# Clustered attention and the small MLP: one joined program, and an opening in a new order

## The chip, the cores and the metric

The kernel runs on one core of one Trainium2 chip. The metric is the time of the device in microseconds (us). Before the change it is 1465.72 us, the median of three runs (1465.66 to 1467.35).

The five engines of the core work side by side, each through its own list of instructions in order: TensorE (PE), VectorE (DVE), ScalarE (ACT), GpSimd (POOL) and SyncE (SP), which only issues DMAs here. They wait for each other by semaphores.

## The reference

The input is 8 batches of 512 tokens with 128 features. Two blocks follow each other.

```python
x = x + attn_block(layernorm(x))           # block 1, on the normalised input n
# inside: n1 = layernorm(n, ln1); q, k, v = n1 @ Wq, Wk, Wv   (16 heads of 8)
#   qb, kb = softmax(q @ Whq), softmax(k @ Whk)               (32 clusters)
#   a = softmax(q k^T / sqrt(8) + 0.1 * qb kb^T) v @ Wo + n
#   a + relu(layernorm(a, ln2) @ W1 + b1) @ W2 + b2           (the small MLP, 512 wide)
x = x + local_ffn(layernorm(x))            # block 2, two layers of windowed
#   attention (8 heads of 64, window 64, rotary) and a gated MLP
```

## The kernel before, in words

`build` calls three stages: `clustered_attention`, `mlp_and_turn` and `local_layers`. Each is a block of its own: every engine has to end its list of one block before any of them begins the next.

**Clustered attention.** A tile is 128 tokens of all features, a batch is 4 tiles. All engines walk the same slots, from -59 to 265 (`over_slots`). A batch has 32 slots of attention; in slot n ScalarE takes one exponential of 128x1024 scores (L670, unit n of 256), TensorE makes the scores of unit n+1 (L410) and the preliminary scores of unit n+12 (L430), of which VectorE takes row maxima (L618), and every second slot TensorE weights the values (L444). The scores have one pair of PSUM banks, so exponential n and scores n+1 take turns. Beside it each tile is prepared in 8 slots: normalise (`scale_input`, GpSimd L751), transpose, project q, k, v (L462) and the two products with the cluster weights (L467), softmax over the clusters, and a split of each number into a leading and a remaining half-precision part, written to `stack_tok` (L782 to L791 on GpSimd; for the queries of the first four tiles `whole_query_chain` on VectorE, L571 to L591). Four transposing DMAs per tile (L827) bring `stack_tok` to `stack`, in the order of `STACK_PARTS`: first half of the heads of the keys, of the queries, then the second halves. `stack_tok` is a single buffer: the next tile's split waits for these DMAs. The first preliminary scores wait for the keys' first half of four tiles and the queries' of three. Small products share three PSUM banks, the bench, in the order of `BENCH_ORDER`.

**The opening.** SP loads the 8 batches of X and then 19 weights, and TensorE waits for all of them before it folds the hash weights into `w_cl` (L378). VectorE takes the statistics of all 32 tiles first (L514, L517). `standardise` (ACT, L658) writes the normalised Z of tiles 4 to 31 in the slots -55 to -28.

**The small MLP.** `mlp_and_turn` works by whole batches: centre (ACT L980), transpose (PE L1049), first product (L1057), ReLU (ACT L995), second product (L1066), addition and statistics (DVE L931 to L946), square root (ACT L1002), normalise (ACT L1010), transpose back (PE L1076) and copy to XT (ACT L1016). Its SP list loads the tables and the first layer's weights of the local stage. The hidden values have four PSUM banks, the outputs two.

## Time and profile before

| what | before |
|---|---|
| median of three runs | 1465.72 us |
| time of the profiled execution | 1465.65 us |
| its span, first to last instruction | 1463.8 us |
| TensorE busy | 1268.3 us, 87% |
| VectorE busy | 1090.7 us, 75% |
| ScalarE busy | 998.3 us, 68% |
| GpSimd busy | 822.2 us, 56% |
| first preliminary scores of a batch | at 70.80 us |
| block of the small MLP begins and ends | 621.77 and 702.2 us |

Busy time is the sum of an engine's instructions, and its share is taken over the whole span; a stage in which the engines wait for each other shows only in a view cut by time. The 1.85 us between the profiled execution's time and its span lie before the first and after the last instruction.

### The profile page before, as it was taken

How to read it: one execution, taken by the hardware profiler on the slowest of the kernel's cores; microseconds unless marked ns; L12 is line 12 of the kernel's file. 1: busy time of each engine (PE TensorE's matmuls, PEld its weight loads, DVE VectorE, ACT ScalarE, POOL GpSimd, SP SyncE). 2: the span in 40 equal slices, each digit the busy share in tenths (PEclk: the TensorE clock that was granted, in tenths of full speed). 3: DMA queues.
4: the chain of work that ended last, by engine and by line, in shares of the span. 5: the costliest groups of instructions: out<-in, count | busy, mean ns of one | idle time of the engine just before them, and what ended most of it. 6: DMA issues, size and time to landing. Idle time of an engine off the chain costs nothing.

```text
span 1463.8 us, 27861 instructions
## 1 busy us (share of the span) xinstructions
PE 1268.3 (87%) x9636; PEld 643.2 (44%) x9636; DVE 1090.7 (75%) x1943; ACT 998.3 (68%) x2313; POOL 822.2 (56%) x1005
## 2 busy tenths in 40 slices
PE   3378989998998988679589999998988999999898
PEld 1112222222222322157256666665534666666554
DVE  4778888888888877223489999995447999999644
ACT  4236766676666666577488999985337999999632
POOL 3666666667766640022577888870028888877200
PEclk9659999999999999989799999999999999999999
DMA  3523333343334330010111111110101111111001
GB/s 103 110 42 65 73 59 65 60 79 58 66 58 73 65 59 1 1 57 1 37 26 27 27 30 27 28 27 2 47 15 42 31 30 27 27 27 31 1 17 41
DMA packets 161120, 60.87 MB, mean 42 GB/s; under 512 B 139691, under 2 KB 152789, under 8 KB 160981
## 3 DMA queue, kind: packets, MB, share of 16 engines
q1 hardware_dynamic: 160980, 59.09, 19.1%
q8 instruction: 78, 1.28, 0.4%
q14 instruction: 62, 0.50, 0.1%
HBM read 8.60 MB, written 2.10 MB: 7 GB/s over the span
## 4 chain that ended last, share of the span: by engine, by line
PE 29%; ACT 11%; DVE 7%; issue 4%; POOL 2%; ACTq 0%; DVEq 0%; POOLq 0%
ACT la_s L1735 8%; PE la_ring L1360 6%; PE la_ring L1372 3%; PE la_s L1393 3%; PE la_pT L1467 3%; DVE la_prob L1624 2%; PE la_pT L1406 2%; PE la_m L1539 2%; PE la_ring L1455 1%; PE la_pT L1457 1%; PE la_s L1455 1%; PE la_s L1457 1%; ACT la_v_own L1777 1%; PE la_s L1385 1%; PE la_o L1422 1%
## 5 line engine op out<-in xcount | busy, mean ns | idle before, releaser
L618 DVE TENSOR_REDUCE row_max<-max_ps 128x2 f32<-128x1024 f32 x256 | 312.9, 1222 | 70.6 <-PE max_ps L430 69.2
L670 ACT ACTIVATE prob<-scores_ps 128x1024 f32<-128x1024 f32 x256 | 262.2, 1024 | 147.8 <-PE scores_ps L410 144.3
L1735 ACT ACTIVATE la_s<-la_s,la_bias,la_inv 128x128 f32<-128x128 f32 x512 | 223.4, 442 | 7.0 <-DVE la_bias L1612 7.0
L1886 POOL TENSOR_TENSOR la_turned<-la_raw,lw_rot 128x1024 f32<-128x1024 f32 x64 | 150.9, 2358 | 115.6 <-PE la_ring L1372 70.1
L1360 PE MATMUL la_ring<-lw_wqkv,la_hT 128*128 128x512 f32 x384 | 202.4, 638 | 15.3 <-DVE la_swapped L1587 6.7
L410 PE MATMUL scores_ps<-stack 128*128 128x512 f16 x512 | 155.7, 386 | 42.0 <-ACT prob L670 41.1
L1892 POOL TENSOR_TENSOR la_turned<-la_turned,la_swapped 128x1024 f32<-128x1024 f32 x64 | 150.7, 2355 | 5.0
L444 PE MATMUL heads_ps<-prob,v_pad 128*32 128x512 f32 x1024 | 137.2, 608 | 1.1 <-ACT prob L670 1.1
L430 PE MATMUL max_ps<-stack 24*128 24x512 f16 x512 | 102.5, 397 | 31.2 <-DVE row_max L618 18.5
L410 PEld LDWEIGHTS scores_ps<-stack 128*128 128x128 f16 x512 | 34.2, 97 | 208.7 <-ACT prob L670 161.3
L1587 DVE TENSOR_TENSOR la_swapped<-la_ring,lw_rot 128x256 f32<-128x256 f32 x256 | 90.8, 415 | 33.3 <-ACT la_raw L1746 23.8
L1735 ACT ACTIVATION_READ_ACCUMULATOR la_s<-la_s,la_bias,la_inv 128x1 f32 x512 | 110.9, 217 | 0.0
L776 POOL TENSOR_TENSOR cl<-cl,cl_inv 128x512 f32<-128x512 f32 x60 | 63.0, 1050 | 85.1 <-DVE cl_inv L559 85.1
L1372 PE MATMUL la_ring<-mlp_ident,la_turned 128*128 128x128 f32 x512 | 82.5, 285 | 12.9 <-DVE la_swapped L1587 11.9
L1360 PEld LDWEIGHTS la_ring<-lw_wqkv,la_hT 128*128 128x128 f32 x384 | 65.4, 197 | 63.8 <-issue 40.0
L1624 DVE TENSOR_TENSOR la_prob<-la_s,la_inv_sum 128x512 f32<-128x512 f32 x128 | 88.5, 691 | 4.8 <-DVE la_inv_sum L1620 0.5
L1406 PE MATMUL la_pT<-mlp_ident,la_prob 128*128 128x128 f32 x512 | 78.6, 276 | 10.5 <-DVE la_prob L1624 8.4
L1372 PEld LDWEIGHTS la_ring<-mlp_ident,la_turned 128*128 128x128 f32 x512 | 58.6, 143 | 61.6 <-ACT la_qT L1759 23.8
L960 POOL TENSOR_TENSOR mlp_base<-X,Z 128x512 f32<-128x512 f32 x8 | 10.2, 1270 | 132.6 <-POOLq L257 87.9
L1746 ACT ACTIVATE la_raw<-la_ring 128x512 f32<-128x512 f32 x128 | 70.6, 589 | 19.0 <-PE la_ring L1360 17.4
L767 POOL TENSOR_TENSOR cl_half<-cl 128x256 f32<-128x256 f32 x60 | 44.0, 733 | 69.4 <-ACT cl L703 69.4
L467 PE MATMUL bench<-w_cl,xnT 128*128 128x512 f32 x128 | 77.7, 694 | 4.6 <-ACT xnT L675 4.1
(177 smaller groups left out, 2765.7 us busy)
## 6 DMA issues: line engine op xcount, KB each, us to landing
la_v_back<-la_v_own SPq DMA_DIRECT2D x112, 128.0 KB, 2.3
X<-in_x SPq DMA_DIRECT2D x8, 256.0 KB, 5.4
stack<-stack_tok SPq DMA_TRANSPOSE x128, 3.2
out<-X SPq DMA_DIRECT2D x8, 256.0 KB, 2.3
lw_wqkv<-in_wqkv SPq DMA_DIRECT2D x2, 768.0 KB, 4.8
stack<-shift_row SPq DMA_DIRECT2D x64, 2.0 KB
lw_rot<-in_rot SPq DMA_DIRECT2D x2, 512.0 KB, 6.5
lw_w<-in_fw SPq DMA_DIRECT2D x2, 341.0 KB
```

The costliest lines, as they stand in the source:

```text
L410: mm = nc.tensor.matmul(scores_ps[:, i, :], stack[:, par, 1, h, kt * P:(kt + 1) * P], stack[:, par, 0, h, :], start=True, stop=True)
L430: mm = nc.tensor.matmul(max_ps[:, e, :], stack[rows, b % 2, 0, 2 * pair + e, qt * P:(qt + 1) * P], stack[rows, b % 2, 1, 2 * pair + e, :], ...
L444: mm = nc.tensor.matmul(heads_ps[32 * j:32 * j + 32, :], v_pad[:, par, kt, 4 * g + j, :], prob[:, c % 4, j, :], start=(kt == 0), stop=(kt ...
L618: nc.vector.tensor_reduce(row_max[:, grp % 2, w // 2, :, w % 2], max_ps[:], AX.X, ALU.max).then_inc(max_made, 1)
L670: nc.scalar.activation(prob[:, c % 4, 2 * pr:2 * pr + 2, :], scores_ps[:], ACT.Exp, scale=1.0 / LOGIT_SCALE).then_inc(exp_made, 1)
L1360: mm = nc.tensor.matmul(ring_ps[:, r % 2, :], hT[:, b % 2, t * P:(t + 1) * P], wqkv[:, at:at + INNER], start=True, stop=True)
L1372: mm = nc.tensor.transpose(ring_ps[:, r % 2, c * P:(c + 1) * P], turned[:, T % 2, SIDE[use], c * P:(c + 1) * P], ident[:])
L1406: mm = nc.tensor.transpose(pT_ps[:, j, :], prob[:, T % 2, j, :], ident[:])
L1624: nc.vector.tensor_tensor(prob[:, T % 2, heads], s_ps[:, heads], inv_sum[:, heads].unsqueeze(2).to_broadcast([P, 4, KEYS]), ALU.mult).then ...
L1735: ins = nc.scalar.activation(s_ps[:, place(h), :], s_ps[:, place(h), :], ACT.Exp, bias=bias[:, T % 2, h:h + 1], scale=inv[:, T % 4, h:h + ...
L1886: nc.gpsimd.tensor_tensor(spun, raw[:, T % 2].rearrange("p s (h f) -> p s h f", f=LD), rot[:, T % TPB, :, 0, :].unsqueeze(2).to_broadcast( ...
L1892: nc.gpsimd.tensor_tensor(turned[:, T % 2], turned[:, T % 2], swapped[:], ALU.add).then_inc(added_rot, 1)
```

## The change

The small MLP is no longer a block. Its pieces run in the list of clustered attention: one batch per 7 slots, from slot 226 on (`mlp_at`), past the last slot of attention to slot 309. Its buffers lie in the half of `stack` that batch 6 has left, its PSUM banks are those that attention leaves: bench banks 1 and 2 (from slot 223 the bench's own uses keep to bank 0), then those of the row maxima, the scores and the heads. The square root of the two inner normalisations becomes a power of -0.5 on GpSimd. The two tables and the q, k, v weights of the first local layer are loaded in the opening.

In the opening the first batch goes ahead: SP loads batch 0, the four weights of the fold, six weights, and only then the other batches and the rest. VectorE takes the statistics of batch 0, then of batches 1 to 3, and of 4 to 7 after the first tile's cluster scores; `standardise` moves to slots -31 to -4. For the first four tiles ScalarE scales the input and writes the leading parts of keys and queries, VectorE and GpSimd write the rests, the queries' half a tile period later than the keys', and the four DMAs go keys, keys, queries, queries.

```diff
 FIRST_STEP, LAST_STEP = -10, 18
 FIRST_SLOT = FIRST_STEP - LEAD_PREP
-LAST_SLOT = B * SLOTS + 10
+LAST_SLOT = B * SLOTS + 16
+MLP_SLOT = B * SLOTS - 30
+MLP_STEPS = 7
+ONE_BANK = MLP_SLOT - 3
+MC = MLP // P
...
 STACK_PARTS = ((1, 0), (0, 0), (1, 1), (0, 1))
-BENCH_ORDER = {}
+FIRST_PARTS = ((1, 0), (1, 1), (0, 0), (0, 1))
+BENCH_BANKS = 3
+BENCH_ORDER, BENCH_BANK, BENCH_BEFORE, BENCH_LAST = {}, {}, {}, {}
 for _n in range(FIRST_SLOT, LAST_SLOT):
     for _u in (*bench_uses(_n)[0], *bench_uses(_n)[1]):
         BENCH_ORDER[_u] = len(BENCH_ORDER)
-BENCH_LIST = list(BENCH_ORDER)
-BENCH_BANKS = 3
+        _banks = BENCH_BANKS if _n < ONE_BANK else 1
+        BENCH_BANK[_u] = BENCH_ORDER[_u] % _banks
+        BENCH_BEFORE[_u] = BENCH_LAST.get(BENCH_BANK[_u])
+        BENCH_LAST[BENCH_BANK[_u]] = _u
...
-                 (w_qT[:, 0, :], a["wqT"]), (w_qT[:, 1, :], a["wkT"]),
-                 (w_hash[:, 0, :], a["whq"]), (w_hash[:, 1, :], a["whk"]),
-                 (w_o[:], a["wo"]), (ln1[:, 0:1], a["ln1_g"]), (ln1[:, 1:2], a["ln1_b"])] + mlp_loads
+        fold_loads = [(w_qT[:, 0, :], a["wqT"]), (w_qT[:, 1, :], a["wkT"]),
+                      (w_hash[:, 0, :], a["whq"]), (w_hash[:, 1, :], a["whk"])]
+        loads = [(ident[:], a["ident"]), (ln1[:, 0:1], a["ln1_g"]), (ln1[:, 1:2], a["ln1_b"]),
+                 (w_qkv[:, 0, :], a["wq"]), (w_qkv[:, 1, :], a["wk"]), (w_qkv[:, 2, :], a["wv"])]
+        late_loads = [(ident16[:], a["ident16"]), (w_o[:], a["wo"])] + mlp_loads
...
         shift_made = sem("shift_made")
         shift_row_made = sem("shift_row_made")
         shift_placed = sem("shift_placed")
+        mlp_ident, w1, w2, b1, ln2, b2_rows = (weights[x] for x in ("ident", "w1", "w2", "b1", "ln2", "b2_rows"))
...
+        def mlp_at(n):
+
...
+        def h_bank(b, c):
+            if b < 2:
+                return bench_ps[:, 1, :]
+            return max_ps[:, c % 2, :] if b == 2 or c < 2 else scores_ps[:, c % 2, :]
+
+        def o_bank(b):
+            return bench_ps[:, 2, :] if b < 4 else heads_ps[:] if b % 2 == 0 else bench_ps[:, 0, :]
...
         @block.tensor
         def _(pe):
-            pe.wait_ge(w_loaded, 16 * len(loads))
+            pe.wait_ge(fold_loaded, 16 * len(fold_loads))
             for i in range(2):
                 nc.tensor.matmul(max_ps[:, i, :], w_qT[:, i, :], w_hash[:, i, :],
                                  start=True, stop=True).then_inc(folded, 1)
+            pe.wait_ge(w_loaded, 16 * len(loads))
...
+            def first_product(b, c):
+                pe.wait_ge(yT_made, b + 1)
+                if b == 0 and c == 0:
+                    bench_is_read(BENCH_LAST[1])
+                elif b < 2:
+                    pe.wait_ge(h_made, MC * b + c)
+                elif b == 2 and c < 2:
+                    pe.wait_ge(max_made, B * SLOTS)
+                elif b == 3 and c >= 2:
+                    pe.wait_ge(exp_made, B * SLOTS)
+                elif b < 4:
+                    pe.wait_ge(h_made, MC * b + c - 1)
+                else:
+                    pe.wait_ge(h_made, MC * (b - 1) + c + 1)
+                nc.tensor.matmul(h_bank(b, c), w1[:, c * P:(c + 1) * P], yT[:, b % 2, :],
+                                 start=True, stop=True).then_inc(h_filled, 1)
...
+            def second_product(b, half):
+                pe.wait_ge(h_made, MC * (b + 1))
+                if b < 4:
...
+                elif b == 4:
+                    pe.wait_ge(heads_moved, B * 4)
+                elif b == 5:
+                    bench_is_read(BENCH_LAST[0])
+                else:
...
+            def mlp_slot(n):
+                m, k = mlp_at(n)
+                if k == 0 and batch_or_none(m + 1) is not None:
+                    turn_input(m + 1)
+                if k == 0 and batch_or_none(m - 3) is not None:
+                    turn_output(m - 3)
+                if 1 <= k <= MC and batch_or_none(m) is not None:
+                    first_product(m, k - 1)
+                if k > MC and batch_or_none(m - 1) is not None:
+                    second_product(m - 1, k - MC - 1)
...
         @block.vector
...
+
+            def input_stats(b):
...
+                for T in range(b * TPB, (b + 1) * TPB):
+                    nc.vector.bn_stats(in_stats[:, T, :], X[:, T, :]).then_inc(stats_done, 1)
+                for T in range(b * TPB, (b + 1) * TPB):
+                    dve.wait_ge(stats_done, T + 1)
+                    ins = nc.vector.bn_aggr(moments[:, T, :], in_stats[:, T, :])
+                ins.then_inc(moments_done, 1)
+
...
+            input_variance(0, FIRST)
...
-            dve.wait_ge(dev1_done, 1)
-            nc.vector.reciprocal(R1[:], dev1[:]).then_inc(r1_done, 1)
+            input_scale(0, FIRST)
+            for b in range(1, 4):
+                input_stats(b)
...
+            def query_share(x):
+
+                cluster_sum(x, 0)
                 share = share_of(x, 0)
-                dve.wait_ge(cl_exp_made[0], x + 1)
-                nc.vector.tensor_reduce(cl_sum[:, 0, :], cl[:, x % 2, 0].rearrange("p (h n) -> p h n", n=NB), AX.X,
-                                        ALU.add).then_inc(cl_sum_made[0], 1)
-                invert_sum(x, 0)
                 dve.wait_ge(cl_inv_made[0], x + 1)
                 nc.vector.tensor_tensor(share, share, inverse_of(0), ALU.mult).then_inc(cl_share_made[0], 1)
...
+            def query_rest(x):
                 dve.wait_ge(hi_made[0], x + 1)
-                nc.vector.tensor_tensor(in_stack(0, 1, 2 * DH, DH, 1), feat, in_stack(0, 1, DH, DH, 1), ALU.subtract)
-                nc.vector.tensor_tensor(in_stack(0, 0, 2 * NB, NB, 1), pairs(share), in_stack(0, 0, NB, NB, 1),
-                                        ALU.subtract).then_inc(lo_made[0], 1)
+                nc.vector.tensor_tensor(in_stack(0, 1, 2 * DH, DH, 1), features_of(x, 0), in_stack(0, 1, DH, DH, 1),
+                                        ALU.subtract)
+                nc.vector.tensor_tensor(in_stack(0, 0, 2 * NB, NB, 1), pairs(share_of(x, 0)),
+                                        in_stack(0, 0, NB, NB, 1), ALU.subtract).then_inc(lo_made[0], 1)
...
-                    nc.vector.bn_stats(stats[:, t, :], Z[:, t, :])
+                    nc.vector.bn_stats(stats[:, t, :], Z[:, t, :]).then_inc(tok_stats_done, 1)
+                dve.wait_ge(tok_stats_done, (x + 1) * TPB)
+                for t in range(x * TPB, (x + 1) * TPB):
+                    nc.vector.bn_aggr(in_moments[:, t, :], stats[:, t, :]).then_inc(in_moments_done, 1)
...
+            def mlp_slot(n):
+                m, k = mlp_at(n)
+                if k == 1 and batch_or_none(m + 2) is not None:
+                    input_shift(m + 2)
+                if k == 1 and batch_or_none(m - 2) is not None:
+                    output_shift(m - 2)
+                if k == MLP_STEPS - 1 and batch_or_none(m - 1) is not None:
+                    add_second(m - 1)
...
-                        whole_query_chain(x)
-                    elif x is not None:
+                    if x is not None and (task != cluster_sum or side == 1 or x >= TPB):
                         task(x, side)
+                    if task == cluster_subtract and side == 0 and x == 0:
+                        for b in range(4, B):
+                            input_stats(b)
+                for x in range(TPB):
+                    if x == tile_at_step(n, 11 if x == TPB - 1 else 16):
+                        query_share(x)
+                    if x == tile_at_step(n, 12 if x == TPB - 1 else 18):
+                        query_rest(x)
...
+                    input_variance(1, REST)
+                    nc.vector.scalar_tensor_tensor(out=minus_mean[:, REST], in0=moments[:, REST, 0], scalar=-1.0,
+                                                   in1=r0[:, REST], op0=ALU.mult, op1=ALU.mult
...
         @block.scalar
...
+            def input_dev(part, tiles):
+                act.wait_ge(moments_done, (1, B)[part])
+                nc.scalar.activation(dev[:, tiles], moments[:, tiles, 1], ACT.Sqrt, bias=eps[:, 0:1]
+                                     ).then_inc(dev_done, 1)
...
+            def leading_part(x, side):
+
+                act.wait_ge(cl_share_made[side], x + 1)
+                act.wait_ge(qkv_made, x + 1)
+                if x >= 1:
+                    act.wait_ge(stack_made[side, 0], 16 * x)
+                    act.wait_ge(stack_made[side, 1], 16 * x)
+                else:
+                    act.wait_ge(constants_set, 1)
+                share, feat = pairs(share_of(x, side)), features_of(x, side)
+                nc.scalar.activation(in_stack(side, 0, (0, NB)[side], NB, 2),
+                                     share.unsqueeze(3).to_broadcast([P, H // 2, 2, 2, NB]), ACT.Copy)
+                nc.scalar.activation(in_stack(side, 1, (0, DH)[side], DH, 2),
+                                     feat.unsqueeze(3).to_broadcast([P, H // 2, 2, 2, DH]), ACT.Copy
+                                     ).then_inc(hi_made[side], 1)
...
+                if tile_at_step(n, -10) is not None and tile_at_step(n, -10) < TPB:
+                    scale_input(tile_at_step(n, -10))
+                if 0 <= n - FIRST_SLOT - 28 < NT - TPB:
+                    standardise(n - FIRST_SLOT - 28 + TPB)
                 if s["exp"] is not None:
                     exponentiate(s["exp"])
...
+                if tile_at_step(n, 9) == 1:
+                    input_dev(1, REST)
                 if s["out"] is not None:
                     g = s["out"]
...
+                for x in range(TPB):
+                    if x == tile_at_step(n, 11):
+                        leading_part(x, 1)
+                    if x == tile_at_step(n, 12 if x == TPB - 1 else 17):
+                        leading_part(x, 0)
+                if tile_at_step(n, 9) == 1:
+                    input_dev1(1, REST)
                 if s["att_t"] is not None:
                     nc.scalar.activation(att_T[:], filled("att_t", s["att_t"]), ACT.Copy).then_inc(att_T_made, 1)
                 if s["max"] is not None and s["max"] % UNITS == UNITS - 1:
...
+            def centre(b):
+                act.wait_ge(in_shift_done, b + 1)
+                if b == 0:
+                    act.wait_ge(scored, (B - 1) * SLOTS)
+                elif b - 1 > 0:
+                    act.wait_ge(turned, b - 1)
+                for i in range(TPB):
+                    T = b * TPB + i
+                    ins = nc.scalar.activation(y[:, b % 2, i, :], Z[:, T, :], ACT.Identity,
+                                               bias=in_shift[:, T:T + 1], scale=in_inv[:, T:T + 1])
...
+            def hidden(b, c):
+                act.wait_ge(h_filled, MC * b + c + 1)
+                if b - 1 > 0:
+                    act.wait_ge(o_filled, 2 * (b - 1))
+                nc.scalar.activation(hid[:, b % 2, c, :], h_bank(b, c), ACT.Relu,
+                                     bias=b1[:, c:c + 1]).then_inc(h_made, 1)
...
+            def normalise(b):
...
+            def take_turned(b):
+                act.wait_ge(out_turned, b + 1)
+                if b == 0:
+                    act.wait_ge(pv_made, B * 16)
+                nc.scalar.activation(XT[:, b, :], bench_ps[:, 1, :], ACT.Copy).then_inc(XT_made, 1)
...
+            def mlp_slot(n):
+                m, k = mlp_at(n)
+                if k == 1 and batch_or_none(m + 1) is not None:
+                    take_yT(m + 1)
+                if 2 <= k < 2 + MC and batch_or_none(m) is not None:
+                    hidden(m, k - 2)
+                if k == MC and batch_or_none(m - 3) is not None:
+                    take_turned(m - 3)
+                if k == MLP_STEPS - 1 and batch_or_none(m + 2) is not None:
+                    centre(m + 2)
+                if k == MLP_STEPS - 1 and batch_or_none(m - 2) is not None:
+                    normalise(m - 2)
...
         @block.gpsimd
...
+            def invert_input(b):
+                at = slice(b * TPB, (b + 1) * TPB)
+                pool.wait_ge(in_moments_done, (b + 1) * TPB)
+                nc.gpsimd.tensor_tensor(in_var[:, at], in_moments[:, at, 1], mlp_eps[:, 0], ALU.add
+                                        ).then_inc(in_var_done, 1)
+                pool.wait_ge(in_var_done, b + 1)
+                nc.gpsimd.tensor_tensor(in_inv[:, at], in_var[:, at], power[:], ALU.pow).then_inc(in_inv_done, 1)
...
+            def invert_output(b):
...
         @block.sync
...
+            def load_input(b):
                 sp.dma_start(X[:, b * TPB:(b + 1) * TPB, :], x_tiles[:, b]).then_inc(loaded[b], 16)
+
...
+            load_input(0)
+            for dst, src in fold_loads:
+                sp.dma_start(dst, src).then_inc(fold_loaded, 16)
             for dst, src in loads:
                 sp.dma_start(dst, src).then_inc(w_loaded, 16)
+            for b in range(1, B):
+                load_input(b)
+            for dst, src in late_loads:
+                sp.dma_start(dst, src).then_inc(late_loaded, 16)
+            for dst, src in early_loads:
+                sp.dma_start(dst, src).then_inc(early_loaded, 16)
...
+                for i, step in enumerate((12, 14, 16, 18)):
+                    x = tile_at_step(n, step)
+                    if x is not None:
+                        turn_stack(x, *(FIRST_PARTS if x < TPB else STACK_PARTS)[i])
 
```

## Rows read from the trace of the kernel before

**Rows 1.** The page's slices: granted TensorE clock, in tenths of full speed.

```profile
PEclk9659999999999999989799999999999999999999
```

**Rows 2.** Busy time by stretch: length, each engine's busy time (instructions), clock, DMA share, GB/s.

```profile
60.00:80.00 20.00, 8.51 (x17) 1.87 (x16) 14.39 (x24) 3.26 (x7) 8.33 (x12) 0.59 0.50 93
...
559.00:594.00 35.00, 28.97 (x181) 8.57 (x183) 24.70 (x30) 21.50 (x27) 0.00 (x0) 1.00 0.00 1
594.00:614.00 20.00, 12.99 (x78) 2.75 (x70) 0.55 (x2) 13.07 (x14) 0.00 (x0) 1.00 0.00 1
614.06:621.77 7.71, 3.45 (x24) 1.96 (x24) 2.11 (x7) 1.19 (x2) 0.00 (x0) 1.00 0.00 0
621.77:637.80 16.03, 8.00 (x16) 3.90 (x17) 3.40 (x36) 9.34 (x19) 5.01 (x4) 0.57 0.40 129
637.80:695.40 57.60, 57.60 (x359) 44.21 (x359) 19.16 (x77) 45.70 (x96) 15.25 (x12) 1.00 0.00 1
695.40:702.50 7.10, 2.16 (x13) 1.34 (x10) 2.29 (x11) 4.09 (x11) 0.00 (x0) 0.71 0.00 1
```

**Rows 3.** Timeline of the opening: start, length, instruction, [idle before <- what ended it].

```profile
15.72 0.43 SPq L813 DMA_DIRECT2D mlp_b_rows<-in_mlp_b_rows  x1
17.94 3.78 PE L378 MATMUL max_ps<-w_hash,w_qT 128*128 128x512 f32 x4 [17.94 <-DMA mlp_b_rows<-in_mlp_b_rows]
21.75 1.08 ACT L652 ACTIVATE w_cl<-max_ps 128x512 f32<-128x512 f32 x2 [3.31 <-PE max_ps L378]
25.05 0.69 DVE L542 TENSOR_REDUCE cl_max<-bench 128x16 f32<-128x512 f32 x1 [6.23 <-PE bench L467]
```

**Rows 4.** Timeline of the third tile's preparation, to the fourth's first instruction.

```profile
48.41 0.68 DVE L542 TENSOR_REDUCE cl_max<-bench 128x16 f32<-128x512 f32 x1
...
52.42 0.63 DVE L571 TENSOR_REDUCE cl_sum<-cl 128x16 f32<-128x512 f32 x1
...
53.69 1.38 POOL L782 CAST stack_tok<-cl 128x1024 f16<-128x1024 f32 x1
...
55.50 1.34 POOL L789 TENSOR_TENSOR stack_tok<-cl,stack_tok 128x512 f16<-128x512 f32 x1
...
58.17 0.68 DVE L542 TENSOR_REDUCE cl_max<-bench 128x16 f32<-128x512 f32 x1
```

**Rows 5.** Timeline: the first preliminary scores.

```profile
70.80 0.61 PE L430 MATMUL max_ps<-stack 24*128 24x512 f16 x2 [7.66 <-DMA stack<-stack_tok]
```

**Rows 6.** The transposing DMAs of 30 to 100 us, by their line.

```profile
L827 SPq DMA_TRANSPOSE stack<-stack_tok x20: 1232/1328/1362, 37.7 to 93.7; - x20
...
DMA to landing us min/median/max: 3.0/3.3/3.9
```

**Rows 7.** Groups to 702 us: instructions, count, busy, mean ns.

```profile
L514 DVE BATCH_NORM_STATS2 in_stats<-X 128x6 f32<-128x128 f32 x32 | 8.3, 265 | 3.3 <-DMA X<-in_x 3.2
```

**Rows 8.** Timeline: nine exponentials in a row late in attention, first and last.

```profile
576.87 1.02 ACT L670 ACTIVATE prob<-scores_ps 128x1024 f32<-128x1024 f32 x1 [1.27 <-PE scores_ps L410]
...
592.00 1.02 ACT L670 ACTIVATE prob<-scores_ps 128x1024 f32<-128x1024 f32 x1 [1.26 <-PE scores_ps L410]
```

**Rows 9.** Timeline: one batch of the small MLP, and one normalisation on ScalarE.

```profile
658.40 1.64 ACT L1010 ACTIVATE mlp_w<-X,mlp_out_shift,mlp_out_inv 128x128 f32<-128x128 f32 x4
...
660.15 0.60 PE L1076 MATMUL mlp_turn_ps<-mlp_ident,mlp_w 128*128 128x128 f32 x4
...
661.02 3.60 PE L1057 MATMUL mlp_h_ps<-mlp_yT,mlp_w 128*128 128x512 f32 x8
...
664.46 3.73 PE L1066 MATMUL mlp_o_ps<-mlp_w,mlp_hid 128*128 128x128 f32 x32
...
668.03 0.60 PE L1076 MATMUL mlp_turn_ps<-mlp_ident,mlp_w 128*128 128x128 f32 x4
```

**Rows 10.** ScalarE's groups, whole span: one of six table loads.

```profile
L703 ACT ACT_TABLE_LOAD x1 | 1.3, 1283 | 0.0
```

**Rows 11.** Timeline: a small GpSimd instruction.

```profile
723.75 0.21 POOL L1871 TENSOR_TENSOR la_newton<-la_inv 128x16 f32<-128x16 f32 x1
```

585 lines of the change are left out of this document (263 added, 322 removed).

## The prediction

> **What bounds the kernel now.** I read the page's slices first, because the shares over the whole span hide stages. TensorE's granted clock is low in three places: the opening, between the stages in the middle, and shortly after [rows 1]. The change touches the first two, so I cut the span by stages [rows 2] and read the timeline in both. The local stage, from 702.5 us on, is over half of the span; of it the change moves only some loads.
>
> The opening is a chain through all engines. TensorE does nothing until the last of 27 loads, issued at 15.72, has landed at 17.94; the cluster weights are ready at 22.83, and VectorE takes the first tile's first maximum at 25.05 [rows 3]. Then one tile follows the other every 9.76 us [rows 4], although no engine is full: at 60 to 80 us TensorE is busy for 8.51 of 20 us, at 0.59 of its clock [rows 2]. The first preliminary scores come at 70.80 and waited for a transposing DMA [rows 5]. Everything of clustered attention hangs on that moment.
>
> In late attention a slot takes 1.89 us (eight slots from 576.87 to 592.00) [rows 8]; it is bound by the turns of ScalarE and TensorE over one pair of score banks, with TensorE idle for 6.0 of 35 us and then for 7.0 of 20 us [rows 2]. At 614.06 the last slot's products begin; until 621.77 there is only the tail of batch 7, TensorE busy for 3.45 us. From 621.77 to 637.80 the MLP starts up at a clock of 0.57, and from 637.80 to 695.40 TensorE is busy all the time at full clock: the stage's body is bound by it [rows 2]. A batch takes 668.03 - 660.15 = 7.88 us: first product 3.44, second 3.57, the two transposes 0.87 together [rows 9]. Last comes a ramp-out of 7.1 us at 0.71 [rows 2].
>
> **The opening, part by part.** Fold and first weights are now DMAs 2 to 11. 15.72 us over 26 issues is 0.60 each, and the last one landed 2.2 us after its issue [rows 3]; so the fifth DMA, which the fold waits for, lands at 5.3 by issue alone, and I take 6.4, since five large transfers share the engines. That is 11.5 us earlier. Three small ScalarE instructions and a transpose now stand between the cluster weights and the first maximum, where they were done in the shade of the DMAs. Each costs between 0.21 [rows 11] and 0.69 [rows 4], 0.8 to 2.8 together; I take 1.3. The first maximum comes at 25.05 - 11.5 + 1.3 = 14.8, a gain of 10.2.
>
> VectorE keeps the statistics of batches 4 to 7 in its list, but now behind the first tile's subtraction: 16 x 0.265 = 4.2 us [rows 7] on the path, as the first tile's sum is queued behind it.
>
> For the tiles after it the old loop is in VectorE's list: from the whole sum at 52.42 to the next tile's maximum at 58.17, 5.75 us of query chain with its waits [rows 4]. It goes to ScalarE (leading parts) and to a later slot. What is late next is the single `stack_tok`: keys' leading part on ScalarE (I take GpSimd's 1.38 for the same elements [rows 4]), rest on GpSimd (1.34 [rows 4] and about 0.6 for its small twin), two DMAs, the second issued 1.33 after the first and landed 3.3 later [rows 6], together 4.6, and 0.3 of handing over: 8.2 us. Below it would be VectorE's own 6.5 or so, above it the old 9.76. ScalarE also carries the 28 `standardise` now beside these tiles, and in tile 1 the square roots of the other 28 tiles: two more table loads of 1.28 each [rows 10], as the exponentials go on before and behind. I take 8.8 for a plain tile, 9.6 for the one with the table loads, and 9.1 for the first (4.9 before its neighbour may start, and 4.2 of statistics): 27.5, against 58.17 - 25.05 = 33.1 before. From the fourth tile's first maximum to the first preliminary scores it was 12.6 (70.80 - 58.17); the keys now pass a longer way (subtraction, VectorE's share of the tile before, GpSimd, ScalarE, GpSimd, DMA), which I sum to 16.1, 3.5 more. Opening: 10.2 + 5.6 - 3.5 = 12.3, taken as 12; first preliminary scores at 58.8. The ends: 16, if a tile takes the 8.2 of the buffer loop and the last way 14; 6, if periods stay at 9.76.
>
> The Trainium skill (ScalarE: Activation LUTs, section on table sets) speaks against this part: exponential and square root are in different sets and should be batched. It gives some 2.7 us per load; the row shows 1.28, and the row decides. By the page's figure the two loads cost 5.3 instead of 2.6, and the opening's gain would be near 10.
>
> **The MLP, part by part.** Its TensorE work to the end of the last second product is 8 x (3.44 + 3.57) + 14 transposes of 0.435 = 62.2 us [rows 9] (the last two transposes back lie in the ramp-out). By slot 256 the new list has done five transposes in, one back, 3.5 first products and two second ones: 2.6 + 12.0 + 7.1 = 21.8.
>
> How much longer do slots 225 to 256 get? TensorE's idle time from 559 to 614 is 13.0 us [rows 2]. If all of it is filled, the stretch grows by 21.8 - 13.0 = 8.8: the floor. Products of 0.86 (a quarter of 3.44) or half second products of 1.79 fit well, as they run while ScalarE takes the exponential of 1.02 [rows 8]. ScalarE's blocks don't: five centrings and one normalisation of 1.64 each [rows 9] stand between two exponentials, where the turn leaves it 1.89 - 1.02 = 0.87 [rows 8], some of that used for shifts and heads. Each adds 0.8 to 1.1, I take 1.0, together 6.0. ReLUs of 0.69 fit in the turn. So 14.8. The upper end is that nothing overlaps: 21.8 + 6.0, near 28.
>
> Behind slot 256 there remain 40.4 us of MLP and 3.45 of attention's tail [rows 2] on TensorE. The tail's waits are now filled, and the transpose in of batches 3 to 6 uses the bank of the outputs until VectorE has added them: 0.9 each (0.69, the size of [rows 4]'s maximum, and a handing over), three of them, 2.7, and 1.5 for waits of the tail in TensorE's list: 4.2. Together 14.8 + 40.4 + 3.45 + 4.2 = 62.9 us from old 614.06 to the end of the last second product, against 695.4 - 614.06 = 81.3: a gain of 18.4. It is the start-up at half clock [rows 2] that goes: TensorE has no gap in front of the MLP, so its clock should stay at 2.4 GHz. The ramp-out stays at 7.1, with a power and an addition on GpSimd in the place of ScalarE's root and VectorE's reciprocal. No row has a power; 0.21 for a small GpSimd instruction [rows 11] and 1.38 for a large one [rows 4] bound it, and I take 0.3 more per pass, counted once: 18.1.
>
> Elsewhere: four aggregations on VectorE and two small GpSimd instructions per batch of attention, in seven batches, next to 1.9 us slots; 0 to 3 us, I take 1.0. The weights loaded early cost nothing, SP and the DMA engines being free there; the tables loaded at the start of the local stage are wanted some 25 us later.
>
> **Sum.** 1465.65 - 12 - 18.1 + 1.0 = **1436.6 us**. The profiled execution is 0.07 below the median and 1.85 over its span; both are kept.
>
> **Rivals.**
> *The opening is bound by ScalarE.* Its list now holds scaling, exponentials, both leading parts, `standardise` and tables, in order; each wait for a DMA holds the next tile's exponential. For it: `stack_tok`'s DMAs land 3.3 us after issue [rows 6]. Against: ScalarE is busy for 3.26 of 20 us there [rows 2]. Periods stay near 10, the gain of the opening falls to 5: 1443.6.
> *The joined slots pack badly.* TensorE's list is in order, so a product that waits for a ReLU holds the scores. Growth of 28: 1449.8. Against: batches 0 and 1 share one hidden bank, but a ReLU ends as the next exponential may begin.
> *They pack well*, growth near the floor of 8.8 and DMAs that land early: 1428.
> *The other side: table loads between exponential and ReLU.* Each of the 13 ReLUs of slots 235 to 256 stands between exponentials. If they need different tables, each costs two loads, 2.57 [rows 10], 33 us in all, and 1470 comes out, slower. It decides from 23 loads on. For it: in the trace no ReLU runs under the exponential's table. Against: in 702 us there are only loads for square root and exponential, though copies and scalings run under both.
> The Trainium skill (ScalarE: Activation LUTs, section on table sets) says that cheap functions such as relu and copy are filler in every set. By that rule this rival falls; the rows agree for the copies and cannot show it for ReLU.
> *It doesn't overlap at all*, because an engine's order holds the MLP behind slot 256: then only the opening's gain and the half-clock start-up remain, 1447; no order in the lists speaks for it.
>
> **Chances.** Forecast with its surroundings (1430 to 1443) 0.58; opening bound by ScalarE 0.15; bad packing or none 0.12; good packing 0.08; table loads 0.04; rest 0.03. About 0.2%, 3 us, is what can be told from no change. Faster 0.92, within 0.2% 0.03, slower 0.05. Range: from the floor of the packing with the best opening, 1425, to bad packing with the forecast's opening, 1451.
>
> **What the new profile would show.** The fold begins at 6 to 7 us; first maximum near 15; first preliminary scores near 59; tiles 8 to 9 us apart. Two more table loads for roots in the opening, none in the joined slots. From slot 225 to 256 some 15 us longer than before; no half clock there; steps of 7.9 to 8.8 us behind it; the local stage begins some 30 us earlier than 702.5 and then runs the same 761 us. It is wrong if the joined slots show a ScalarE that switches tables, a tile period near 10, or a local stage that is longer.

## The result, and the profile after

| | before | changed |
|---|---|---|
| median, 4 runs each | 1466.28 us | 1441.97 us (1439.89 to 1443.88) |
| profiled execution, its span | 1465.65, 1463.83 us | 1443.05, 1441.26 us |

The ratio is 0.9833, 95% interval 0.9816 to 0.9850: 24 us faster, 5.4 above the forecast of 1436.6 and inside its range. A second measurement of the same kernel, in another group of runs, gave 0.9825 (0.9808 to 0.9842). All times compared here are of undisturbed executions; the single other one, 2099.94 us at a mean granted clock of 0.552 (of the version without the power), is left out.

I cut both traces at the same events, each stretch from the start of one instruction to the start of the next one named. Lengths in us; the last two columns belong to the experiments below.

| stretch | before | changed | forecast of the change | measured | three edits |
|---|---|---|---|---|---|
| start to first row maximum | 71.44 | 58.80 | -12 | -12.6 | 58.51 |
| to the first exponential | 24.48 | 24.47 | 0 | 0 | 24.47 |
| exponential 0 to 224 | 459.69 | 461.46 | +1.0 | +1.8 | 461.10 |
| 224 to 255 (joined slots) | 57.38 | 75.85 | +14.8 | +18.5 | 71.42 |
| 255 to the end of the MLP | 89.24 | 57.02 | -32.9 | -32.2 | 54.69 |
| local stage | 761.61 | 763.66 | 0 | +2.0 | 761.10 |

The granted clock of the changed kernel, by slices, against [rows 1]: the half-clock stretch between the stages is shorter, and it is still there.

```profile
PEclk9579999999999999998799999999999999999999
```

Busy time by stretch, as in [rows 2] (length, then the engines' busy times, clock, DMA share, GB/s): tile preparation; joined slots; behind them to the last second product; ramp-out; start of the local stage.

```profile
30.00:50.00 20.00, 9.04 (x15) 3.90 (x14) 14.42 (x29) 18.24 (x38) 8.78 (x11) 0.67 0.68 125
544.73:620.58 75.85, 64.24 (x376) 25.85 (x375) 33.28 (x57) 54.73 (x83) 7.45 (x8) 1.00 0.00 1
620.58:668.40 47.82, 46.47 (x296) 34.94 (x294) 19.22 (x69) 33.49 (x65) 21.62 (x25) 1.00 0.00 1
668.40:677.90 9.50, 2.26 (x9) 1.43 (x8) 2.81 (x11) 4.52 (x11) 3.17 (x4) 0.62 0.00 1
677.90:700.40 22.50, 14.16 (x15) 4.52 (x16) 8.69 (x25) 6.56 (x11) 11.95 (x11) 0.50 0.29 75
```

The MLP's start-up at clock 0.57 [rows 2] is gone: in this trace the clock is 1.00 from the joined slots to the last second product, and TensorE is busy for 46.47 of the last 47.82 us. The opening, in the timeline of the changed kernel, against [rows 3] and [rows 5]:

```profile
6.36 3.78 PE L425 MATMUL max_ps<-w_hash,w_qT 128*128 128x512 f32 x4 [6.36 <-DMA w_hash<-in_whk]
...
13.24 1.49 PE L513 MATMUL bench<-w_qkv,xnT 128*128 128x384 f32 x2
...
16.48 0.69 DVE L674 TENSOR_REDUCE cl_max<-bench 128x16 f32<-128x512 f32 x1 [3.44 <-PE bench L518]
...
24.60 0.63 DVE L674 TENSOR_REDUCE cl_max<-bench 128x16 f32<-128x512 f32 x1
...
33.85 0.68 DVE L674 TENSOR_REDUCE cl_max<-bench 128x16 f32<-128x512 f32 x1
...
43.04 0.68 DVE L674 TENSOR_REDUCE cl_max<-bench 128x16 f32<-128x512 f32 x1
...
58.15 0.61 PE L481 MATMUL max_ps<-stack 24*128 24x512 f16 x2 [6.54 <-DMA stack<-stack_tok]
```

The fold starts as forecast. The steps from tile to tile are 8.1, 9.25 and 9.2 us, 26.6 against a forecast of 27.5 and 33.1 before [rows 3, 4]. The last way, from 43.04 to 58.15, is 15.1 instead of 16.1. The steps of the small MLP behind the joined slots, from the end of one batch's second product to the next, are 11.2, 9.8, 9.0, 8.1 and 7.4 us, where I had written 7.9 to 8.8.

### The profile page after: what moved, and what is told of

Same layout as the page of the kernel before. It is cut to its first block, busy times and chain, and to the rows that moved or that the text cites. A ratio compares the mean times of both kernels' runs of the same rounds, so it can differ in the third digit from the quotient of the medians.

```text
span 1441.3 us, 27920 instructions
## 1 busy us (share of the span) xinstructions
PE 1268.8 (88%) x9636; PEld 643.8 (45%) x9636; DVE 1084.5 (75%) x1927; ACT 1007.7 (70%) x2327; POOL 824.9 (57%) x1020
## 3 DMA queue, kind: packets, MB, share of 16 engines
q8 instruction: 78, 1.28, 0.4%
## 4 chain that ended last, share of the span: by engine, by line
PE 29%; ACT 11%; DVE 8%; issue 4%; POOL 2%; ACTq 0%; DVEq 0%; POOLq 0%
ACT la_s L1859 8%; PE la_ring L1480 6%; PE la_ring L1492 3%; PE la_s L1515 3%; PE la_pT L1589 3%; DVE la_prob L1748 2%; PE la_pT L1528 2%; PE la_m L1663 2%; PE la_ring L1577 2%; PE la_s L1579 1%; PE la_pT L1579 1%; PE la_s L1577 1%; ACT la_v_own L1901 1%; PE la_s L1507 1%; PE la_o L1544 1%
## 5 line engine op out<-in xcount | busy, mean ns | idle before, releaser
L495 PE MATMUL heads_ps<-prob,XT 128*32 128x512 f32 x1024 | 137.9, 611 | 0.0
L1492 PE MATMUL la_ring<-mlp_ident,la_turned 128*128 128x128 f32 x512 | 81.9, 283 | 12.6 <-DVE la_swapped L1711 11.6
L1528 PE MATMUL la_pT<-mlp_ident,la_prob 128*128 128x128 f32 x512 | 78.7, 276 | 11.8 <-DVE la_prob L1748 10.3
L1730 DVE TENSOR_REDUCE la_neg_max<-la_s 128x8 f32<-128x1024 f32 x64 | 77.8, 1216 | 5.4 <-PE la_s L1515 5.4
L481 PEld LDWEIGHTS max_ps<-stack 24*128 24x128 f16 x512 | 24.4, 91 | 128.4 <-DVE row_max L785 85.3
L1528 PEld LDWEIGHTS la_pT<-mlp_ident,la_prob 128*128 128x128 f32 x512 | 59.5, 141 | 49.4 <-DVE la_prob L1748 38.6
```

Source lines behind the costliest of these rows:

```text
L481: mm = nc.tensor.matmul(max_ps[:, e, :], stack[rows, b % 2, 0, 2 * pair + e, qt * P:(qt + 1) * P], stack[rows, b % 2, 1, 2 * pair + e, :], ...
L495: mm = nc.tensor.matmul(heads_ps[32 * j:32 * j + 32, :], v_pad[:, par, kt, 4 * g + j, :], prob[:, c % 4, j, :], start=(kt == 0), stop=(kt ...
L1492: mm = nc.tensor.transpose(ring_ps[:, r % 2, c * P:(c + 1) * P], turned[:, T % 2, SIDE[use], c * P:(c + 1) * P], ident[:])
L1528: mm = nc.tensor.transpose(pT_ps[:, j, :], prob[:, T % 2, j, :], ident[:])
```

## The joined slots, read

TensorE's groups between exponentials 224 and 255, before (555.61 to 612.98 us) and changed (544.73 to 620.58): count, busy, mean ns, idle time before them and what ended it.

```profile
L410 PE MATMUL scores_ps<-stack 128*128 128x512 f16 x62 | 18.7, 384 | 12.5 <-ACT prob L670 11.9
L444 PE MATMUL heads_ps<-prob,v_pad 128*32 128x512 f32 x128 | 17.0, 604 | 0.0
```

```profile
L459 PE MATMUL scores_ps<-stack 128*128 128x512 f16 x62 | 18.7, 383 | 7.3 <-ACT prob L890 7.1
L495 PE MATMUL heads_ps<-prob,XT 128*32 128x512 f32 x128 | 17.0, 605 | 0.0
L582 PE MATMUL bench<-stack,mlp_w 128*128 128x512 f32 x16 | 8.6, 619 | 3.4 <-ACT stack L985 3.4
L597 PE MATMUL bench<-mlp_w,stack 128*128 128x128 f32 x64 | 7.8, 275 | 0.0
L481 PE MATMUL max_ps<-stack 24*128 24x512 f16 x40 | 7.8, 384 | 0.5 <-DVE row_max L785 0.5
```

Before, TensorE was busy for 44.55 us and idled 12.8, nearly all of it in front of the scores. Now it idles 75.85 - 64.24 = 11.6: only 5.2 us of the wait for the exponential are filled, and 3.4 of a new wait stand beside it. That is a first product waiting for the ReLU that empties the one hidden bank of batches 0 and 1. A centring is seen from both sides at 563 us:

```profile
562.40 0.60 PE L459 MATMUL scores_ps<-stack 128*128 128x512 f16 x2
...
563.02 1.63 ACT L970 ACTIVATE stack<-Z,mlp_in_shift,mlp_in_inv 128x128 f32<-128x128 f32 x4
...
564.56 1.00 ACT L890 ACTIVATE prob<-scores_ps 128x1024 f32<-128x1024 f32 x1
...
565.62 0.60 PE L459 MATMUL scores_ps<-stack 128*128 128x512 f16 x2 [2.30 <-ACT prob L890]
```

The scores lie ready from 563.0, and the exponential starts when the centring ends.

So the growth of 18.5 us is 64.24 - 44.55 = 19.7 of additional work, less only 1.2 of idle time that went. The work is as priced: up to here the list has done twelve first products, four half second ones and four and a half transposes (16 + 8, 64 and 18 matmuls), by the prediction's prices 12 x 0.86 + 2 x 3.57 + 4.5 x 0.435 = 19.4.

```profile
L582 PE MATMUL max_ps<-stack,mlp_w 128*128 128x512 f32 x8 | 4.1, 592 | 0.0
L565 PE MATMUL bench<-mlp_ident,stack 128*128 128x128 f32 x18 | 2.8, 274 | 0.4 <-DVE X L753 0.4
```

What went otherwise is the idle time. My theory was that order and blocks, not TensorE's capacity, made the growth 18.5. The rival was capacity: in a slot that also weights values, TensorE must pass 0.39 + 1.06 + 0.60 us in front of the next exponential anyway, and each piece of MLP comes on top of it.

## Experiments

**The opening alone.** The new opening, with the old separate MLP behind attention.

```diff
+        mlp_and_turn(nc, a, X, Z, stats, mlp_w, [], XT)
...
-                mlp_slot(n)
```

> The new opening alone; behind attention stands the old, separate small MLP (the first local weights are still loaded in the opening). If the two parts of the change add up, as the prediction has it, the first preliminary scores stay near 58.2 us, the first exponential is 12.7 us earlier than in the kernel before, and the whole takes 1465.7 - 12.7 = 1453 us; the MLP's half-clock start-up of 16 us comes back. Rival: the earlier start only moves a wait (late attention or the local stage gives part of it back), as the changed kernel's local stage was 2 us longer: then 1455 to 1457.

Measured: 1452.60 us, ratio 0.9913 (0.9896 to 0.9931), 12.7 us less by the ratio (11.8 by the medians: before was 1464.42 in that group); first exponential at 81.96. The opening gives its whole gain alone. What is left to the joined MLP is 11.7 us (0.9833 against 0.9913), a difference: no run has it without the new opening. The steady slots took 460.57 us here, 0.9 more than before, although this version has none of the aggregations and small GpSimd instructions beside attention.

**TensorE makes the preliminary scores first.**

```diff
                 if s["max"] is not None:
                     make_max_scores(s["max"])
+                mlp_slot(n - 1)
...
-                mlp_slot(n)
+                else:
+                    mlp_slot(n - 1)
```

> In the joined slots TensorE makes the next preliminary scores first and the piece of MLP behind them, where the changed kernel does it the other way round; nothing else differs. Theory (order): the first products cost some 3.7 us per batch in the joined slots because they stand before the preliminary scores, so that the row maxima, the shift, the ReLU behind it and with them the one hidden bank of batches 0 and 1 come late. Then the joined slots grow by 10 to 14 us and not by 18.5, and the time is 4 to 8 us shorter than the changed kernel's 1442, near 1436. Rival (capacity): TensorE is simply full in these slots, and the order is worth less than 1 us: 1441 to 1442.

Measured: 1438.01 us, 0.9812 (0.9786 to 0.9837); joined slots 75.22, only 0.6 shorter. That length hides the edit's effect:

```profile
543.73:618.95 75.22, 66.45 (x376) 26.46 (x375) 33.15 (x57) 54.90 (x82) 7.46 (x8) 0.98 0.00 1
```

TensorE idles 75.22 - 66.45 = 8.8 us instead of 11.6, so the order takes 2.8 us of idle time away. But the same 376 instructions keep it busy for 66.45 instead of 64.24, with a short fall of the clock among them (0.76 and 0.82 in 562 to 570 us, 1.00 in the changed kernel). Against the 4 to 8 us expected it is a miss, and capacity alone (under 1 us) doesn't describe it either.

**Joined 8 slots later.**

```diff
-MLP_SLOT = B * SLOTS - 30
+MLP_SLOT = B * SLOTS - 22
```

> The joined MLP begins 8 slots later (234 instead of 226). The changed kernel's growth up to exponential 247 was 12.7 us, so the joined slots should now grow by about 12.7 instead of 18.5, while 8/7 of a batch step of 7.88 us, 9.0, moves behind slot 256: 3.2 us slower than the changed kernel, near 1445. Rival: the slots joined last cost as much as they hide (TensorE is full there, one microsecond grown for each one moved): no difference, 1442. If all of a step's work were hidden free, it would be 9 slower: 1451.

Measured: 1445.46 us, 0.9867 (0.9846 to 0.9889), 5 us slower than the changed kernel by the ratios. The joined slots grew by 12.7, as expected from the growth up to exponential 247. The part behind came out 12.05 longer, 69.07 instead of 57.02, and not 9.0: the first steps behind slot 256 are the slow ones (10.8 and 9.8 us, 8.1 and 7.4 at the end). So the last eight joined slots cost 75.85 - 70.07 = 5.8 us and save 12; full as TensorE is there, joining pays. The 5.8 is too low: this version has a short half-clock spell in the joined slots (0.57 in 579 to 583 us), the changed kernel none. Two such spells lengthened the repeat of the changed kernel by 2.9 us (last section), so I estimate 7.2 us at full clock, and a growth of 11.3 instead of 12.7.

**GpSimd adds X and Z a step earlier, behind the output shift.**

```diff
+                    pool.wait_ge(out_shift_done, b - 1)
...
-                if k == 2 and batch_or_none(m - 1) is not None:
-                    add_base(m - 1)
+                if k == 2 and batch_or_none(m) is not None:
+                    add_base(m)
```

> GpSimd adds X and Z for a batch one MLP step earlier, and only once VectorE has made the output shift of the batch two before. Theory: in the changed kernel these additions stand beside VectorE's small output shift and stretch it from 0.16 to 1.2 us, and the last batch's sum comes 1.4 us late for VectorE's last addition. Both go: the shift is 0.16 in the ramp-out, the last addition follows the second product at once, and the time from slot 256 to the end of the MLP is 2 to 3 us shorter: 1439 to 1440. Rival: the shift's 1.2 us is its own when its input has just been written by GpSimd; then it stays at 1.2 with nothing beside it, and only 1.4 us go.

In the changed kernel, at the end of the MLP (start, length, instruction, idle before it):

```profile
666.83 1.02 POOL L1125 TENSOR_TENSOR mlp_out_inv<-mlp_out_var,mlp_power 128x4 f32<-128x4 f32 x1
667.82 1.26 POOL L1111 TENSOR_TENSOR stack<-X,Z 128x512 f32<-128x512 f32 x1
...
667.88 1.22 DVE L769 SCALAR_TENSOR_TENSOR mlp_out_shift<-mlp_out_moments,mlp_out_inv 128x4 f32<-128x4 f32 x1 [1.41 <-POOL mlp_out_inv L1125]
...
670.53 0.69 DVE L753 TENSOR_TENSOR X<-bench,stack 128x512 f32<-128x512 f32 x1 [1.42 <-POOL stack L1113]
```

and in this one:

```profile
666.05 0.16 DVE L769 SCALAR_TENSOR_TENSOR mlp_out_shift<-mlp_out_moments,mlp_out_inv 128x4 f32<-128x4 f32 x1 [1.41 <-POOL mlp_out_inv L1126]
```

Measured: the part behind exponential 255 takes 54.95 instead of 57.02, 2.07 less, and the shift is 0.16 for each of the eight batches, where the changed kernel has 1.22 to 1.24 for seven and 0.16 for the last: the 1.2 us came from GpSimd's addition beside it, and the rival falls. The 2.07 lie wholly behind the last second product (7.10 instead of 9.17). The time was 1436.28 us (0.9804, 0.9777 to 0.9830), by the ratios 4 us below the changed kernel (the intervals overlap), 2 more than the edit explains; see the last section.

**Centring on GpSimd.**

```diff
-                if k == MLP_STEPS - 1 and batch_or_none(m + 2) is not None:
-                    centre(m + 2)
...
+                    ins = nc.gpsimd.tensor_scalar(y[:, b % 2, i, :], Z[:, T, :], in_inv[:, T:T + 1],
+                                                  in_shift[:, T:T + 1], ALU.mult, ALU.add)
...
+                if k == 2 and batch_or_none(m + 2) is not None:
+                    centre(m + 2)
```

> The input of the MLP is centred by GpSimd (idle in the joined slots) instead of ScalarE; the rest as in the changed kernel. Theory (blocks): a centring of 1.64 us on ScalarE stands between the scores and the next exponential, which in the slot at 563 us starts 1.5 us late with TensorE idle for 2.3; five such blocks cost 5 x 1.5, so the joined slots grow by 11 to 12 us and not by 18.5, and the time is 6 to 8 us shorter than the changed kernel's 1442. By the price in the prediction (1.0 each) it is 5 us. Rival (capacity): TensorE's own work grew by 19.7 us in these slots and sets their length; the time won at the blocks is lost again at the next products: 0 to 2 us.

Measured: 1437.78 us, 0.9821 (0.9806 to 0.9835); joined slots 73.53, at clock 1.00. Five blocks were worth 2.3 us together, about 0.5 each, neither 1.5 nor my 1.0. The wait before the scores fell by 2.1, the wait for the ReLU stayed at 3.4. TensorE's idle time went from 11.6 to 73.53 - 64.04 = 9.5. Why a block that delays its own exponential by 1.5 costs 0.5 in the end wasn't measured; that the following slots make it good is my reading.

**The other tiles' roots on GpSimd.**

```diff
-                    input_dev(1, REST)
...
-                    input_dev1(1, REST)
...
+                    nc.gpsimd.tensor_tensor(R1[:, REST], dev1[:, REST], rest_power[:], ALU.pow).then_inc(r1_done, 1)
...
+                        nc.gpsimd.tensor_tensor(r0[:, REST], dev[:, REST], rest_power[:], ALU.pow
+                                                ).then_inc(r0_done, 1)
```

> The square roots for tiles 4 to 31 in the opening are made by additions and powers on GpSimd, so that ScalarE needs no table of the square root between its exponentials. If the two table loads of 1.28 stand on the path of the second tile, as the prediction has it, the first preliminary scores come 2.6 us earlier, less what powers of 128x28 on GpSimd cost (1.02 for 128x4; 1 to 3 if it grows with size, behind the keys' rest of the first tile): -2.6 to 0 against the changed kernel. Rival: the loads are hidden behind the DMAs that each tile waits for: no difference, or up to 2 us slower through the powers.

GpSimd's groups (count, busy, mean ns):

```profile
L1139 POOL TENSOR_TENSOR mlp_out_inv<-mlp_out_var,mlp_power 128x4 f32<-128x4 f32 x8 | 8.1, 1016 | 0.6
L1045 POOL TENSOR_TENSOR R<-in_dev,rest_power 128x28 f32<-128x28 f32 x1 | 4.8, 4815 | 0.1
L1108 POOL TENSOR_TENSOR in_r<-in_dev,rest_power 128x28 f32<-128x28 f32 x1 | 4.8, 4805 | 0.1
```

Measured: 1448.62 us, 0.9890 (0.9875 to 0.9904), 8 us slower than the changed kernel, outside both theories. Two powers of 4.8 us stand in GpSimd's list ahead of the tiles; their steps become 12.0 and 14.1, and the first row maximum comes 6.8 us later (65.56). The joined slots took 80.47 at a mean clock of 0.94, with the same 11.6 us of idle time, and the local stage 760.4. This is a finding on powers and says nothing of the table loads.

**The same roots left out, copies in their place.**

```diff
-                nc.scalar.activation(dev[:, tiles], moments[:, tiles, 1], ACT.Sqrt, bias=eps[:, 0:1]
+                nc.scalar.activation(dev[:, tiles], moments[:, tiles, 1], (ACT.Sqrt, ACT.Identity)[part],
```

> Leaves a part of the computation out: for tiles 4 to 31 the two square roots in the opening are replaced by plain copies with the same bias (the instructions stay, the table loads go). If the two loads of 1.28 are on the second tile's path, as the prediction has it, the step from the second tile's first maximum to the third's falls from 9.25 to about 6.7 and everything behind is 2.6 us earlier: 1439.5. Rival: that step is set by the way through the single buffer and its DMAs, and the loads lie in ScalarE's idle time: 9.2 stays, 1442.

Measured: second to third tile's maximum 7.96 instead of 9.25, and first maximum to first row maximum 40.3 instead of 42.3. So two loads of 1.28 cost 2.0 on the path, 1.3 of it in the third tile's step, which was expected to fall to 6.7; the rival, by which nothing changes, falls. In the time (1440.14 us, 0.9832, 0.9815 to 0.9848) 2 us don't stand out.

**VectorE's statistics behind the first sum.**

```diff
-                    if task == cluster_subtract and side == 0 and x == 0:
+                    if task == cluster_sum and side == 1 and x == 0:
```

> VectorE's statistics of batches 4 to 7 (4.2 us) come behind the first tile's sum over the keys' clusters instead of ahead of it. By the prediction they stand on the first tile's path and the opening gets 4.2 us shorter (1438 in all). Rival: the second tile's first maximum came 8.1 us behind the first's all the same, so the statistics lie beside the preparation of the second tile, and what they delay is only the first tile's way to its single buffer, which may be caught up later: 0 to 2 us.

Measured: 1441.57 us, 0.9846 (0.9829 to 0.9862), no difference. From the first tile's maximum to the first row maximum it is 41.4 instead of 42.3. The version with four edits below has 41.8, and the nine with the statistics in the old place and the roots on ScalarE 42.0 to 42.4. The 4.2 us of statistics were 0.9 at most on the path: the rival holds.

**Three edits together, and four.** Preliminary scores first, the early addition, centring on GpSimd; then the statistics' place too.

> Three edits together: preliminary scores ahead of the MLP's piece, GpSimd's addition of X and Z a step earlier, centring on GpSimd. If they act in different places they add up: joined slots 8 to 9 us shorter than the changed kernel's 75.9 (one for the order, 7.5 for the blocks), the part behind slot 256 2.1 us shorter (57.0 to 54.9), so some 10 us below the changed kernel, near 1431. If centring on GpSimd lengthens what VectorE does beside it or GpSimd itself becomes late (it then has 6.4 us of work in steps of 7.9), 3 to 5 us of it are lost.

> The three edits before (1433.1) and the statistics of batches 4 to 7 behind the first tile's sum. The statistics were worth 0.9 us in the steps between the tiles' first maxima when alone, so 1432; that is the best version if the gain is real. If the statistics were worth nothing in the time, as their three rounds say (1441.6 against 1442.0), 1433.

The joined slots with three edits, and two of TensorE's groups in them:

```profile
544.09:615.51 71.42, 64.78 (x376) 25.77 (x375) 31.91 (x56) 47.48 (x63) 16.98 (x27) 1.00 0.00 1
```

```profile
L459 PE MATMUL scores_ps<-stack 128*128 128x512 f16 x62 | 18.7, 383 | 4.9 <-ACT prob L892 4.9
...
L583 PE MATMUL bench<-stack,mlp_w 128*128 128x512 f32 x16 | 8.9, 639 | 1.3 <-ACT stack L975 1.2
```

Measured: three edits 1433.12 us (1431 expected), 0.9786 (0.9771 to 0.9800); four 1433.32 us, 0.9781 (0.9765 to 0.9797). These are the best versions: four edits are 7.0 us below the changed kernel of the same group (below), 8 to 10 were expected, and the fourth edit adds nothing that can be told. The joined slots take 71.42 (71.43 with four edits), 4.4 less than 75.85, half of the 8 to 9 expected. It is more than the lengths of the single edits, 0.6 + 2.3, but the idle times add up: 2.8 for the order and 2.1 for the centring make 4.9, and TensorE idles 71.42 - 64.78 = 6.6 us instead of 11.6. So the order takes the same idle time away alone as beside the others; in its own run the fall of the clock hid it. In length it is worth 73.53 - 71.42 = 2.1 us beside the centring, at full clock. The wait for the ReLU goes from 3.4 to 1.3.

**The changed kernel again, and the power left out.**

> The changed kernel unaltered, on the same chip as the others of this group. 1440 to 1444, the version with four edits 8 to 10 us below it. Its local stage took 763.7 us in the first profile, 758.6 to 761.6 in seven others with the same local stage: it should come out between 758 and 762 here; if it is 763 again, the edits do something to the local stage that I don't see.

> Leaves a part of the computation out: with the three edits, the power that inverts the output deviations (1.02 us for 128x4 on GpSimd) is replaced by a product. If it counts once, in the ramp-out, as the prediction has it, the part behind slot 256 falls from 54.7 to 53.9, 0.8 us in all: 1432.3. Rival: each batch's normalisation waits for it and ScalarE's blocks come later in each step behind slot 256: 5 x 0.8, 4 us: 1429.

```diff
-                nc.gpsimd.tensor_tensor(out_inv[:, par], out_var[:, par], power[:], ALU.pow).then_inc(out_inv_done, 1)
+                nc.gpsimd.tensor_tensor(out_inv[:, par], out_var[:, par], power[:], ALU.mult).then_inc(out_inv_done, 1)
```

Measured: the changed kernel 1440.31 us with a local stage of 761.25, inside the expected 758 to 762 (of the seven others that I had counted there, one was 762.0). Without the power 1432.14 us, 0.9769 (0.9753 to 0.9785), and the part behind exponential 255 takes 53.89, 0.80 less than with three edits, about as much as one power takes longer than one product (1.02 and 0.20 us): it counts in the ramp-out alone.

## Why the prediction was right, and where it was off

The forecast of the profiled execution was 6.45 us too low (1436.6 against 1443.05). By the stretches of the first table: joined slots +3.7, local stage +2.0, steady slots +0.8, MLP behind them +0.7, opening -0.6. The range was kept, but several sizes in it cancelled, as told below.

*Opening, right in sum.* Fold at 6.4 as taken. The first maximum came at 16.48, not 14.8; its products ran at half-clock length (last section). The steps of the tiles were 0.9 better than forecast and the last way 1.0. Inside, terms were wrong in size and cancelled, which is luck: the first step was put at 4.9 and 4.2 of statistics; without the statistics ahead of it it still takes 7.8 to 8.1, and they cost 0.9 at most in all. The table loads are in the sum with 0.8 (9.6 against 8.8 for a plain tile); 2.0 of their 2.57 are on the path. ScalarE's timeline in the changed kernel shows that a switch is the load and nothing more:

```profile
27.50 1.13 ACT L923 ACTIVATE cl<-cl 128x512 f32<-128x512 f32 x2
28.65 1.28 ACT L832 ACT_TABLE_LOAD   x1
29.95 0.32 ACT L832 ACTIVATE in_dev<-in_moments,in_eps 128x28 f32<-128x28 f32 x1
```

By the 2.7 us of the Trainium skill (ScalarE: Activation LUTs, section on table sets) two would have cost 5.3; measured between the neighbours it is 1.32 each.

ScalarE is busy for 18.24 of 20 us in this stretch, and taking the loads from its list shortened a step, so ScalarE is on the path, as the rival had it; but its steps of 10 us did not come. What sets the 9.2 of a plain tile was not separated.

*Joined slots, mechanism right, two terms mis-sized.* The step "products of 0.86 or half second products of 1.79 fit well" failed. TensorE's 13.0 us of idle time were to be filled whole and 6.0 added for blocks, so 6.0 should be left; 11.6 were, 5.6 more. 5.2 of the old wait for exponentials were filled, 7.3 stayed, and the wait for the one hidden bank, that I named in a rival as harmless, is 3.4. On the other side the work was 19.7 and not 21.8 us: I had counted 3.5 batches of first products, and by the start of exponential 255 it is three. The two together make 18.5 instead of 14.8. ScalarE's blocks, charged at 6.0, were too dear: five of the six gave 2.3 back when they left. The rival of bad packing (28) is refuted, and so is good packing.

*Table loads between exponentials and ReLUs.* There is none in the joined slots, which hold 32 exponentials and 12 ReLUs; the rule of the Trainium skill (ScalarE: Activation LUTs, section on table sets), by which relu and copy are in every set, agrees with this trace.

*Behind slot 256, right in sum.* From the end of exponential 255 to the end of the last second product 46.8 us against 48.05. TensorE is busy for 45.48 of them, idle for 1.35: the waits, charged at 4.2, were too dear, and the work, 40.4 + 3.45, too small, as two first products more were left over. The ramp-out was 9.2 instead of 7.4: the power costs 1.02, where I took 0.3 more per pass, and the addition's place cost 1.42 at the last batch, a wait I hadn't seen. Both are shown by experiments (0.80 and 2.07). The clock kept 1.00 in front of the MLP, as forecast; in the repeat of the changed kernel it fell twice in the joined slots (last section).

*Elsewhere.* The steady slots cost 0.5 to 1.8 us in the twelve traces of kernels with the joined MLP, against my 1.0; the changed kernel's 1.8 holds a spell at clock 0.57 in 520 to 524 us. The version with the opening alone took 0.9 more without the aggregations, so that they cost the 1.0 isn't shown. The local stage's 2.0 is no effect of the change: it took 758.6 to 763.7 us in the thirteen traces with the new opening, and before's 761.6 lies among them.

## What to carry to other kernels

Filling an engine's idle time with another stage's work pays even where it seems full (each joined slot cost 0.7 to 0.9 us and saved 1.5), but here half of the idle time was left even in the best version. Compare each piece with the gap of its own slot and not with the mean. Put pieces behind the instruction that others wait for, and blocks on an engine that is idle there; read what such an edit is worth from busy and idle time and not from the length alone, in which a fall of the clock can hide it. Price an operation that no row shows by its worst bound when it stands in a ramp-out.

## What the runs showed of the hardware

A power on GpSimd costs 1.02 us for 128x4 and 4.8 for 128x28; a plain operation on 128x4 there costs 0.20. A VectorE instruction on 128x4 took 1.22 to 1.24 us instead of 0.16 while GpSimd added two arrays of 128x512 in SBUF.

The changed kernel took 1437.1 to 1443.9 us in eight runs. Its two traces differ by 1.5 us in the opening, 2.9 in the joined slots and 2.4 in the local stage, not all the same way, and in each the half-clock stretches differ; the other six runs have no trace. In the opening the first q, k, v product (384 columns, two matmuls) shows it: 1.49 us in the changed kernel (above), as long as the 1.51 of the same product at 39.16, where the granted clock is 0.50. (For 12 to 17 us the view of the clock says 1.00, so here half clock is read from the length alone.) In the version with the statistics moved it is shorter:

```profile
12.69 0.82 PE L513 MATMUL bench<-w_qkv,xnT 128*128 128x384 f32 x2
```

The first maximum comes at 14.41 instead of 16.48 there; in the five traces with a product of 0.82 it comes at 14.4 to 15.1, in the six with 1.49 at 15.9 to 16.5. In the repeat of the changed kernel the clock fell right behind the centring of 563 us, where TensorE is idle for 2.30 (the row of the changed kernel stands above, at 1.00 throughout):

```profile
560.00:564.00 4.00, 1.70 (x13) 0.34 (x6) 3.16 (x10) 3.40 (x7) 1.76 (x3) 0.90 0.00 0
564.00:568.00 4.00, 4.00 (x21) 2.12 (x20) 1.62 (x3) 1.80 (x2) 1.97 (x2) 0.68 0.00 0
```

The joined slots took 78.70 there instead of 75.85, with the same 11.6 us of idle time: all of the 2.9 is busy time. Of the eight traces with the joined MLP and the centring on ScalarE, four have half clock in the joined slots; of the four with the centring on GpSimd, none has. That fits the idle time as the occasion of it, but eight and four are too few to show it. At the start of the local stage the clock differs too:

```profile
674.00:696.50 22.50, 13.04 (x24) 4.41 (x25) 10.10 (x29) 8.93 (x14) 13.41 (x12) 0.74 0.29 75
```

is the row of the kernel with the early addition, whose local stage took 758.6; the changed kernel has 0.50 over the same length and took 763.7, and so does the version without the roots, also 763.7. What decides whether the clock falls in one execution and not in the next was not settled.
